# Four attentions and a convolution block on one core: an earlier last sum, and normalised quarters spread further apart

## The reference

```python
# layer 0 and layer 2 (eight heads of 32 channels; layer 2 adds to the normalised xn)
xn = group_norm(x)                      # 32 groups of 8 channels
q, k, v = split(qkv_w @ xn + qkv_b)
h = softmax(q.T @ k / sqrt(32)) @ v     # 1024 x 1024 weights for each head
x = x + (proj_w @ h + proj_b)
# layer 1
x1 = group_norm(x) + pos_emb
weights = sigmoid(conv1x1(silu(conv3x3(silu(conv1x1(x1))))))
sh = group_norm(x1)
standard = attention(sh, heads=8)                  # as above
multi = [attention(x1 * weights, sh, 128 channels) for each of 2]
fused = silu(concat(standard, multi) @ ff_w1.T + ff_b1) @ ff_w2.T + ff_b2
x = group_norm(fused @ out_w.T + out_b) + x        # "post" norm, then the residual
# layer 3: group norm, attention with a single head of 256 channels, projection, residual
```

## Time and profile before

| | |
|---|---|
| median of three runs | 5093.48 us (5091.28 to 5097.12) |
| the profiled execution, its own time | 5105.42 us |
| its span, first to last instruction | 5103.6 us |
| PE busy | 4840.6 us (95%) |
| DVE busy | 3041.7 us (60%) |
| POOL busy | 2929.0 us (57%) |
| ACT busy | 2414.5 us (47%) |
| mean granted clock of TensorE | 0.966 of full speed |
| exponential on ACT, 128x512 | 599 ns, 3456 of them |
| maximum on DVE, 128x512 | 681 ns, 3456 |
| addition on POOL, 128x1024 | 2376 ns |
| residual addition on POOL, 128x512 | 1275 ns, 32 |
| scaling on ACT, 128x512 | 811 ns, 192 |
| statistics on DVE, 128x512 | 684 ns, 192 |

### The profile page before, as it was taken

One profiled execution on the slowest core, in us unless ns is written; L12 is line 12 of the kernel. 1 busy time (PEld: TensorE's weight loads), 2 busy tenths in 40 slices (PEclk: granted clock), 3 DMA queues, 4 the chain that ended last, 5 costly groups with the idle time before them and its releaser, 6 DMA issues. The chain is left out here.

```text
span 5103.6 us, 62796 instructions
## 1 busy us (share of the span) xinstructions
PE 4840.6 (95%) x21912; PEld 2221.6 (44%) x21912; DVE 3041.7 (60%) x5400; ACT 2414.5 (47%) x4321; POOL 2929.0 (57%) x1675
## 2 busy tenths in 40 slices
PE   7799999999999999999999999999999999999888
PEld 3335333553336433464334643346334463335434
DVE  6455677366764666636665467655676456773362
ACT  3453565335652455524555245552565425653251
POOL 3353686446863477735776357763677536864351
PEclk8899999999999999999999999999999999999999
DMA  3112121022110221112210112201122012210020
GB/s 90 34 32 63 46 54 39 21 63 57 44 34 28 69 52 46 27 36 57 59 45 21 42 51 60 52 13 48 48 57 57 7 54 59 52 45 11 18 50 13
DMA packets 105142, 223.41 MB, mean 44 GB/s; under 512 B 31616, under 2 KB 33920, under 8 KB 104704
## 3 DMA queue, kind: packets, MB, share of 16 engines
q1 hardware_dynamic: 104832, 219.39, 16.7%
HBM read 56.47 MB, written 8.39 MB: 13 GB/s over the span
## 5 line engine op out<-in xcount | busy, mean ns | idle before, releaser
L911 ACT ACTIVATE probs<-bank 128x512 f32<-128x512 f32 x3456 | 1933.8, 599 | 2322.0 <-PE bank L566 2308.9
L1014 DVE TENSOR_REDUCE max_cols<-bank 128x1 f32<-128x512 f32 x3456 | 2180.7, 681 | 1267.2 <-PE bank L566 1260.7
L1264 POOL TENSOR_TENSOR probs_added<-probs_added,probs 128x1024 f32<-128x1024 f32 x794 | 1858.7, 2376 | 67.3 <-ACT probs L911 66.8
L566 PE MATMUL bank<-q_stack,k_stack 97*128 97x512 f32 (+1 forms) x3584 | 1684.0, 520 | 88.0 <-ACT probs L911 23.7
L566 PE MATMUL bank<-probs,v_tokens 128*32 128x512 f32 (+1 forms) x7168 | 1348.7, 625 | 4.8 <-ACT probs L911 4.8
L566 PEld LDWEIGHTS bank<-q_stack,k_stack 97*128 97x128 f32 (+1 forms) x3584 | 657.5, 193 | 828.7 <-issue 456.6
L1264 POOL TENSOR_TENSOR probs_added<-probs 128x1024 f32<-128x1024 f32 x192 | 453.6, 2373 | 886.5 <-ACT probs L911 886.1
L566 PE MATMUL bank<-act,weight_stream 128*128 128x512 f32 x1792 | 927.6, 617 | 16.0 <-issue 6.9
L1251 POOL TENSOR_TENSOR probs_added<-probs_added,probs 128x512 f32<-128x512 f32 x288 | 368.1, 1278 | 623.9 <-ACT probs L911 622.8
L566 PEld LDWEIGHTS bank<-probs,v_tokens 128*32 128x32 f32 (+1 forms) x7168 | 315.4, 120 | 409.6 <-issue 293.9
L566 PEld LDWEIGHTS bank<-act,weight_stream 128*128 128x128 f32 x1792 | 324.7, 193 | 335.1 <-issue 297.3
(11 more groups left out here) (84 smaller groups left out, 2862.0 us busy)
## 6 DMA issues: line engine op xcount, KB each, us to landing
k_stack<-high_parts SPq DMA_DIRECT2D x384, 128.0 KB, 2.4
q_stack<-high_parts SPq DMA_DIRECT2D x768, 64.0 KB, 2.0
weight_stream<-stream_dram SPq DMA_DIRECT2D x32, 768.0 KB, 4.3
k_stack<-low_parts SPq DMA_DIRECT2D x192, 128.0 KB, 2.4
q_stack<-low_parts SPq DMA_DIRECT2D x384, 64.0 KB, 2.0
act<-x_dram SPq DMA_DIRECT2D x8, 1024.0 KB, 6.4
act<-pos_dram SPq DMA_DIRECT2D x8, 1024.0 KB, 5.4
weight_stream<-stream_dram SPq DMA_DIRECT2D x16, 512.0 KB, 3.8
```

The source lines that it names most:

```text
L566: return nc.tensor.matmul(dst, lhsT, rhs, start=start, stop=stop, **kw)
L911: act.activation(PR[:, PLACE[m], j, :], bank[:, :], ACT.Exp, scale=att.scale).then_inc(reading(key), 1)
L1014: dve.tensor_reduce(cols[:, kh, j, qt:qt + 1], bank[:, :], AX.X, ALU.max).then_inc(reading(key), 1)
L1264: pool.tensor_tensor(ADD[:, js, :], one, two, ALU.add).then_inc(p_added, 1)
```

## The change

Three things are changed. First, in narrow attentions the last sum, the transposition, the inversion and the transposition back of steps 0, 1 and 2 come one unit earlier (35, 36, 36, 36 in place of 36, 37, 37, 37); the normalisation stays at 37. The fourth step, the wide attentions and the amounts are as they were. Second, `norm` has a parameter that sets the distance of the four scalings. It was 4/4.4 = 0.91 units; it is 1.8 for "post" and 1.6 for "2", in the between-work "2" alone. Third, the residual additions there go from 1.2 units apart (from 45.8) to 1.8 apart (from 46.5), the statistics from 1.5 (from 53) to 1.6 (from 53.5), and the norm "2" starts at 60.3, not 59.5.

```diff
-def norm(name, at, lag, src, dst, one=1, late=4.0):
+def norm(name, at, lag, src, dst, one=1, late=4.0, apart=None):
...
-        each("apply", [(name, src, dst) + q for q in QUARTERS], at + 2 * lag + 3 * one + late, late / 4.4)
+        each("apply", [(name, src, dst) + q for q in QUARTERS], at + 2 * lag + 3 * one + late, apart or late / 4.4)
...
-        out += norm("post", 33.3, 2.5, "o", "o") + each("res", QUARTERS, 45.8, 1.2) + \
-            each("stats", [("x",) + q for q in QUARTERS], 53, 1.5) + norm("2", 59.5, 2.3, "x", "m") + \
+        out += norm("post", 33.3, 2.5, "o", "o", apart=1.8) + each("res", QUARTERS, 46.5, 1.8) + \
+            each("stats", [("x",) + q for q in QUARTERS], 53.5, 1.6) + norm("2", 60.3, 2.3, "x", "m", apart=1.6) + \
...
-        ends = (11, 12, 12, 13, 14) if att.wide else (36, 37, 37, 37, 37) if s + 1 < att.steps else (34, 36, 36, 36, 37)
+        ends = (11, 12, 12, 13, 14) if att.wide else (35, 36, 36, 36, 37) if s + 1 < att.steps else (34, 36, 36, 36, 37)
```

## The result

The changed kernel took 5064.45 us (median of five runs, 5056.58 to 5066.73) against 5093.48 us for the kernel before. The ratio is 0.9934, with a 95% interval of 0.9917 to 0.9951. A second set gave 0.9937 (0.9918 to 0.9956). So it is faster by about 30 us, where 12 were forecast; the time lies in the range, but the move is more than twice the forecast. The granted clock over the whole went from 0.966 to 0.978, which the prediction had named as a sign that it is wrong.

A forecast was written before the change was run, and what follows sets the result against it. PE, 95% busy, was taken to set the end, so reordering pays only where PE stands or its clock falls afterwards. Terms -1.8 +5.6 -8.1 -4 -3.5 = -11.8 us from 5093.48 gave 5082 us, range 5061 to 5104.

The forecast's parts named there:

- Part 1: Step ends of narrow attentions: sums one unit earlier, -0.25 us a turn, -1.8 us over seven turns.
- unit 8 starts when it did: Going from step 0 to 1: PE still waits at unit 8 for the normalisation, so 0 for 21 of 63 places.
- Part 2, step 1: Kind 0: later residuals delay statistics and the maxima PE needs, costing +5.6 us over seven turns at full clock.
- the variance product: Kind 0 step 1, unit 30: two operations it needs move one maximum back, making the delay +0.8 instead of +0.5.
- Part 2, step 2: Kind 0: exponentials between scalings remove two PE waits, q projection 1.16 us earlier a turn, -8.1 us over seven.
- The clock: Kind 0: fewer half-clock spells, -4 us in step 2 and -3.5 in step 1; bounds 0 to -27, up to +10.
- PE at half clock runs inside DVE's wait: Kind 0 step 1: reason for counting only a fifth of 18.5 us, -3.5, as clock gain.
- (a): Rival: the clock pays in step 1 of kind 0 too, another -12 us, 5070; chance 0.20.
- (b): Rival: residuals become the bound in step 1 of kind 0, +14 us in all, 5107; chance 0.15.
- (c): Rival: nothing measurable, step 2 gain given back at h_ready or to DVE, 5093; chance 0.27.
- The signs: Trace marks, whole kernel; wrong if statistics row under 20 us, most step 1 passages under 41, or clock moves over 0.005.
- The row of statistics: Whole-kernel DVE waits for POOL's residual additions: 13.6 us growing to over 30; under 20 would mean the prediction is wrong.

The follow-up runs named there:

- the norm 2 alone: Kernel before with only the four scalings of the norm "2" set 1.6 apart, its start left at 59.5; ratio 0.9956 (0.9942 to 0.9970).
- the repeats there: Kernel before with matmuls repeated in kind 0, four at unit 16 of step 1 and three at unit 10 of step 2; 5087.07 us, 0.9981.

## Why the prediction was wrong

- **Part 1, -1.8.** It came to about nothing: the terms were small, as forecast, but "unit 8 starts when it did", waiting for the normalisation, was wrong, and so was one sign. Without spells, the sums alone give about -0.15 us in each of step 1 of kinds 2 and 1 (forecast 0) and step 2 of kind 2 (forecast -0.3), and +0.2 in each of step 3 of kind 2 (forecast +0.25) and step 2 of kind 1 (forecast -0.25: wrong sign); over seven turns about nothing.
- **Part 2, step 1, +5.6.** The chain was right: ACT's first scaling stands 2.03 instead of 1.65 us (0.38; forecast 0.39), the fourth residual comes behind the last addition, DVE waits for residuals 27.8 instead of 13.6 us (forecast over 30, and wrong if under 20). PE meets it at unit 26 rather than 30, with 3.3 us. The rest at equal clock of this edit is +4.0, so the size is near, but partly by luck. By the same line the runs split it into +9.2 for the spread scalings of "post", for which I had a gain of 0.3 a turn that I then left out of the sum, and -5 for the moved residuals and statistics, for which I had charged the 5.6. The working also has a slip: 2423.6 +0.6 +0.6 +0.5 +0.7 is 2426.0, not 2426.6, so the +0.5 was none, and the 0.8 for the variance product, on which the 5.6 rests, is read from no row.
- **Part 2, step 2, -8.1.** Right in kind, too large: 0.2 us a turn in the changed kernel and 0.5 with the norm 2 alone, by the passages without a spell, instead of 1.16 (the rest of the norm 2 alone, -6.8, would be near the 8.1; passages are the more direct reading), since the projection then waits for the bank of the exponential behind the last scaling. "Next is the q projection, which needs all four quarters" left out that it also needs a bank.
- **The clock, -7.5.** This is the step that failed. It measured -31 to -33 by the slope of time against clock, four times as much. I looked for spells only in steps 1 and 2 of kind 0, "with these waits gone I count a good half of it". The table of steps by turn would have shown from the trace of before alone that step 3 of kind 2, step 0 of kind 1 and step 0 of kind 2 stood 36 us above their quickest passages, more than my whole bound of 27 for kind 0. And I treated it as the price of local waits, where an edit that lengthens a wait can take spells away elsewhere by moving them. In step 1 my reason for taking little, "PE at half clock runs inside DVE's wait", was right behind unit 17, as the repeats there showed. No term could have been given for that from one profile; a wider range could.
- **Rivals.** (a) "The clock pays in step 1 too" was nearest in direction, with 5070, but put the gain in the wrong kinds. (b) fell: the residuals are late as it said, and the time fell. (c) fell.
- **The signs.** Exponentials between the scalings, statistics behind residuals, the later shift and the earlier sums all came. The row of statistics, 27.8, lies between the "over 30" and the "under 20". PE still waits 0.26 and 0.57 us for ACT in step 2, where no wait was forecast, and unit 8 no longer waits for the normalisation. Passages of step 1, in the windows of the earlier trace rows, were under 41 us in three turns of seven, not in most. The sign that did say "wrong" was the clock: it moved by 0.012, with 0.005 as the bound. Projections came 0.2 us earlier from the first exponential of the step (14.94 against 15.13, in turns alike in clock), not 1.1.

## What to carry to other kernels

Where a kernel is bound by TensorE at 95% and has short waits, make a table of equal steps by turn first. In this kernel steps that took one of two or three times, with all other engines' work unchanged, had spells of the half clock, and their sum above the quickest was what was at stake. Look then whether PE sets the pace there: behind unit 17 of step 1 the half clock cost nothing, since POOL was never idle. One wait of about 1.3 us in each of seven turns, filled with repeats of the matmul ahead of it, was worth as much here as the whole rearrangement, though only 11 to 18 of the 36 us came at the place itself. A gain of this kind should be tested against a kernel with the waits filled before it is put down to the order, since it hangs on lengths elsewhere and can go with the next edit.

## What was not expected of the hardware

The level of the clock changes on evenly spaced moments that the program doesn't set, and a wait of 1.27 us on PE is followed by the half clock 36 times of 36 when the step starts in one part of the interval and 0 times of 17 in the rest but for its edge (4 of 10). Adding 6.3 us of matmuls to the kernel before changed its time by -2 us, adding 12.7 by +19, though both intervals still hold the plain sum. A stretch of 14.0 us with the same 57 matmuls lasted as long at clock 0.76 as at 1.00. And 28 matmuls that compute nothing new took 36 us off a kernel of 5093.
